# Attention scores on the halves of the PE array: one head of a pair per 64 rows, query-score and key-score matmuls in turn

## The reference

```python
x = x + layernorm(attention(layernorm(x)))      # 16 batches, 256 tokens, 16 heads of width 8
x = x + layernorm(ffn(layernorm(x)))            # 32 experts of width 64, top 6, and a shared one of 256
# attention, for each batch and head:
scores = einsum('bhtd,bhsd->bhts', q, k) / sqrt(8)
out = einsum('bhts,bhsd->bhtd', softmax(scores), v)
```

## Time and profile before

| | |
|---|---|
| timed runs, us | 591.12, 585.29, 587.35 |
| median | 587.35 us |
| profiled execution: span from first to last instruction | 588.6 us |
| instructions in it | 10713 |
| mean granted clock of TensorE | 0.986 of full speed |
| attention with its start, feed-forward layer | about 0 to 305 us, 305 to 588 us |

### The profile page before, as it was taken

The page is one execution under the profiler, slowest core; times in us unless marked ns, Lnnn a source line. Parts: engine busy times, 40 slices in busy tenths (PEclk is TensorE's granted clock), DMA queues, the critical chain, the costliest instruction groups (busy, mean ns, idle before and its releaser), DMA issues.

```text
span 588.6 us, 10713 instructions
## 1 busy us (share of the span) xinstructions
PE 541.1 (92%) x3248; PEld 316.9 (54%) x3248; DVE 423.1 (72%) x1116; ACT 430.1 (73%) x879; POOL 191.2 (32%) x763
## 2 busy tenths in 40 slices
PE   2488979999999999999989999999999999999993
PEld 1234545555555555654446565656566566556551
DVE  6686757789887878768856968695876769487343
ACT  2326757788887987877687687887869687877873
POOL 6241111225153424121103335535363553403030
PEclk9999989999998999999999999999999999999997
DMA  6333364333333233223000000000000000000001
GB/s 176 116 101 93 103 233 130 91 95 104 96 102 110 85 110 108 87 87 95 13 3 1 1 1 1 1 19 1 20 0 19 0 3 18 0 19 1 19 0 36
DMA packets 42776, 33.76 MB, mean 57 GB/s; under 512 B 4032, under 2 KB 35392, under 8 KB 42464
## 3 DMA queue, kind: packets, MB, share of 16 engines
q1 hardware_dynamic: 42720, 33.09, 18.8%
HBM read 18.01 MB, written 14.68 MB: 56 GB/s over the span
## 4 chain that ended last, share of the span: by engine, by line
PE 58%; POOL 11%; DMA 6%; issue 6%; ACT 6%; DVE 6%; SPq 6%; ACTq 0%; POOLq 0%; DVEq 0%
PE pY L1183 8%; PE pS L1183 7%; PE pO L1100 7%; PE pS L1088 6%; PE pS L1077 6%; PE pS L1160 4%; PE pS L1162 4%; PE pS L1161 4%; DMA kp<-k_scratch 4%; PE pS L1169 4%; SPq L369 3%; DMA k_scratch<-k_parts 3%; ACT probs L556 2%; SPq L357 2%; DVE mneg L770 2%
## 5 line engine op out<-in xcount | busy, mean ns | idle before, releaser
L770 DVE TENSOR_REDUCE mneg<-pS 128x2 f32<-128x512 f32 x256 | 164.5, 686 | 39.6 <-PE pS L1077 37.8
L556 ACT ACTIVATE probs<-pS 128x512 f32<-128x512 f32 x256 | 140.9, 599 | 46.9 <-PE pS L1088 46.3
L946 DVE TENSOR_TENSOR h_ring<-pS,rr 128x512 f32<-128x512 f32 x128 | 88.4, 691 | 79.4 <-ACT rr L633 74.5
L1077 PE MATMUL pS<-kp,qp 96*128 96x256 bf16 x512 | 103.8, 288 | 11.5 <-DMA kp<-k_scratch 10.8
L624 ACT ACTIVATE r<-pS 128x512 f32<-128x512 f32 x144 | 84.7, 588 | 29.3 <-PE pS L1162 29.1
L1088 PE MATMUL pS<-qp,kp 102*128 102x512 bf16 x256 | 99.8, 393 | 4.7 <-ACT probs L556 3.0
L633 ACT ACTIVATE rr<-r 128x512 f32<-128x512 f32 x128 | 80.8, 631 | 4.4 <-DVE h_ring L946 0.5
L1160 PE MATMUL pS<-qp,up_hi 128*128 128x512 f32 x144 | 80.6, 560 | 0.9 <-ACT r L624 0.8
L1077 PEld LDWEIGHTS pS<-kp,qp 96*128 96x128 bf16 x512 | 45.6, 101 | 58.3 <-issue 16.6
L1183 PE MATMUL pS<-h_ring,down_sb 128*128 128x512 f32 x144 | 73.4, 591 | 0.0
L1183 PE MATMUL pY<-h_ring,down_sb 128*128 128x512 f32 x144 | 72.9, 591 | 0.0
(11 more groups left out here) (191 smaller groups left out, 802.2 us busy)
## 6 DMA issues: line engine op xcount, KB each, us to landing
qp<-q_scratch SPq DMA_DIRECT2D x64, 96.0 KB
kp<-k_scratch SPq DMA_DIRECT2D x64, 96.0 KB
q_scratch<-q_parts SPq DMA_DIRECT2D x16, 192.0 KB, 2.2
k_scratch<-k_parts SPq DMA_DIRECT2D x16, 192.0 KB, 2.2
q_scratch<-q_parts SPq DMA_DIRECT2D x16, 128.0 KB, 2.1
k_scratch<-k_parts SPq DMA_DIRECT2D x16, 128.0 KB, 2.1
out_x<-ot SPq DMA_DIRECT2D x7, 256.0 KB, 2.3
q_scratch<-q_parts SPq DMA_DIRECT2D x16, 64.0 KB, 1.8
```

What stands on the lines that cost most here:

```text
L556: nc.scalar.activation(probs[j][:, sh], pS2[n % S2_RING][:, :, :], ACT.Exp, scale=SCALE).then_inc(exp_done, 1)
L770: nc.vector.tensor_reduce(mneg[u % 2][:, :, hh, k], pS1[n % S1_RING][:, :].rearrange("p (a s) -> p a s", a=TH), AX.X, ALU.max, negate=True ...
L946: nc.vector.tensor_tensor(h_sb[n % HRING], pC[k % 2], r2_sb[k % 2][:, :], ALU.mult).then_inc(h_done, 1)
L1077: ins = mm(pS1[n % S1_RING][:, T * th:T * (th + 1)], qp[slot][0:2 * QK_ROWS, hh, k, P * th:P * (th + 1)], kp[slot][0:2 * QK_ROWS, k, :], s ...
```

## The change

Each head of a pair gets a half of the array's rows: head 0 rows 0 to 47, head 1 rows 64 to 111 (HALF = 64), with the three rows of its maxima behind them, 51 rows in all. `qp` needs no zeroed copies and shrinks to half. A key-score call now covers one head and both halves of the keys in two matmuls of 256 columns, head 1 first (`KEY_HEADS`), and `probs` is laid out accordingly. In each step of a batch but the last one, `scores_by_both` first makes all waits and then issues four matmuls of 256 columns: query scores of one head, key scores of the other head, and both again. The last batch has key scores alone, and the first two units query scores alone, with the heads in turn. POOL's zeroing of `qp` goes; the ones are now written to 32 partitions in each half, so by two DVE instructions for each `kp` buffer. x_lo moves to `kp`, and x_cut gets a tile of its own.

```diff
-DIFF_ROWS = 2 * QK_ROWS + 2 * M_ROWS
+DIFF_ROWS = QK_ROWS + M_ROWS
+HALF = P // 2
+KEY_HEADS = (1, 0)
...
-        qp = [sb(f"qp{i}", [P, 2, UB, T], BF16) for i in range(RING)]
+        qp = [sb(f"qp{i}", [P, UB, T], BF16) for i in range(RING)]
...
-                    rows = slice(QK_ROWS * hh, QK_ROWS * (hh + 1))
+                    rows = slice(HALF * hh, HALF * hh + QK_ROWS)
...
-            sp.wait_ge(preset, 1)
             sp.wait_ge(ones_set, 1)
...
-            for i in range(RING):
-                ins = nc.gpsimd.memset(qp[i][:, :, :, :].rearrange("p a b c -> p (a b c)").bitcast(F32), 0.0)
-            ins.then_inc(preset, 1)
...
-                for sh in range(TH):
-                    n = TH * (NBLK * b + j) + sh
+                for i, hh in enumerate(KEY_HEADS):
+                    n = 2 * (NBLK * b + j) + i
                     act.wait_ge(s2_done, n + 1)
-                    nc.scalar.activation(probs[j][:, sh], pS2[n % S2_RING][:, :, :], ACT.Exp,
+                    nc.scalar.activation(probs[j][:, hh], pS2[n % S2_RING][:, :, :], ACT.Exp,
...
             for i in range(RING - 1):
-                nc.vector.memset(kp[i][2 * QK_ROWS:P, :, :], 1.0)
+                for hh in range(2):
+                    nc.vector.memset(kp[i][HALF * hh + HALF // 2:HALF * (hh + 1), :, :], 1.0)
...
+            def query_scores(u, k, hh, th):
+                slot, n = u % RING, 2 * (UB * u + k) + hh
+                rows = slice(HALF * hh, HALF * hh + QK_ROWS)
+                return mm(pS1[n % S1_RING][:, T * th:T * (th + 1)], qp[slot][rows, k, P * th:P * (th + 1)],
+                          kp[slot][rows, k, :], start=True, stop=True)
+
+            def key_scores(u, k, i, sh):
+                slot, n = u % RING, 2 * (UB * u + k) + i
+                rows = slice(HALF * KEY_HEADS[i], HALF * KEY_HEADS[i] + DIFF_ROWS)
+                return mm(pS2[n % S2_RING][:, sh], kp[slot][rows, k, P * sh:P * (sh + 1)], qp[slot][rows, k, :],
+                          start=True, stop=True)
...
+            def scores_by_both(uq, uk, k, i):
+
+                query_scores_free(uq, k, i)
+                key_scores_free(uk, k, i)
+                query_scores(uq, k, i, 0)
+                key_scores(uk, k, i, 0)
+                query_scores(uq, k, i, 1).then_inc(s1_done, 1)
+                key_scores(uk, k, i, 1).then_inc(s2_done, 1)
...
                         if not last:
-                            scores_by_query(2 * b + 2 + j // UB, j % UB, hh)
-                        scores_by_key(b, j, hh)
+                            scores_by_both(2 * b + 2 + j // UB, 2 * b + j // UB, j % UB, hh)
+                        else:
+                            scores_by_key(2 * b + j // UB, j % UB, hh)
```

More of the change, by code:

```diff
@@ L150, in block_kernel @@
         mT_sb = [sb(f"mT{i}", [2 * M_ROWS * UB, T], BF16) for i in range(2)]
-        probs = [sb(f"probs{j}", [P, TH, 2, T]) for j in range(NBLK)]
+        probs = [sb(f"probs{j}", [P, 2, TH, T]) for j in range(NBLK)]
         oT_sb = sb("oT_sb", [P, 4, T])
@@ L159, in block_kernel @@
         xT = sb("xT", [P, TILE])
-        x_hi, x_lo = ([qp[i][:, part].rearrange("p a b -> p (a b)").bitcast(F32R) for i in range(2)]
-                      for part in range(2))
-        x_cut = kp[0][:, :, :].rearrange("p a b -> p (a b)").bitcast(F32)
+        x_hi, x_lo = ([ring[i][:, :, :].rearrange("p a b -> p (a b)").bitcast(F32R) for i in range(2)]
+                      for ring in (qp, kp))
+        x_cut = sb("x_cut", [P, TILE])
         e_sb = sb("e_sb", [P, C4, E])
@@ L600, in high_x @@
                     act.wait_ge(up_done, FBLK * (i - 1))
-                copy(x_hi[i % 2], x_cut).then_inc(xhi_done, 1)
+                copy(x_hi[i % 2], x_cut[:, :]).then_inc(xhi_done, 1)
             def high_up(c):
@@ L962, in _ @@
             ins.then_inc(ln1_stats, 1)
-            nc.vector.memset(kp[RING - 1][2 * QK_ROWS:P, :, :], 1.0).then_inc(ones_set, 1)
+            for hh in range(2):
+                ins = nc.vector.memset(kp[RING - 1][HALF * hh + HALF // 2:HALF * (hh + 1), :, :], 1.0)
+            ins.then_inc(ones_set, 1)
             dve.wait_ge(wqk_loaded, 16 * N_WQK)
@@ L967, in _ @@
             dve.wait_ge(wa_loaded, 16 * N_WA)
-            dve.wait_ge(preset, 2)
+            dve.wait_ge(preset, 1)
             keep_v(0)
@@ L1072, in scores_by_query, with query_scores_free @@
+            def query_scores_free(u, k, hh):
+                n = 2 * (UB * u + k) + hh
                 if k == 0 and hh == 0:
-                    pe.wait_ge(packed[slot], 4 * 16 * (u // RING + 1))
+                    pe.wait_ge(packed[u % RING], 4 * 16 * (u // RING + 1))
                 if n >= S1_RING:
                     pe.wait_ge(max_done, n - S1_RING + 1)
-                for th in range(TH):
-                    ins = mm(pS1[n % S1_RING][:, T * th:T * (th + 1)], qp[slot][0:2 * QK_ROWS, hh, k, P * th:P * (th + 1)],
-                             kp[slot][0:2 * QK_ROWS, k, :], start=True, stop=True)
@@ L1079, in scores_by_query, with key_scores_free @@
[L1079 to L1085, removed]
+            def key_scores_free(u, k, i):
+                n = 2 * (UB * u + k) + i
+                if k == 0 and i == 0:
+                    pe.wait_ge(m_packed[u % RING], 2 * 16 * (u // RING + 1))
@@ L1086, in scores_by_key, with scores_by_query @@
                 if n >= S2_RING:
                     pe.wait_ge(exp_done, n - S2_RING + 1)
-                mm(pS2[n % S2_RING][:, :, :], kp[slot][0:DIFF_ROWS, k, P * sh:P * (sh + 1)],
-                   qp[slot][0:DIFF_ROWS, :, k, :], start=True, stop=True).then_inc(s2_done, 1)
+            def scores_by_query(u, k):
+                for hh in range(2):
+                    query_scores_free(u, k, hh)
+                for th in range(TH):
+                    for hh in range(2):
+                        ins = query_scores(u, k, hh, th)
+                        if th == TH - 1:
+                            ins.then_inc(s1_done, 1)
@@ new lines, in scores_by_key @@
+            def scores_by_key(u, k, i):
+                key_scores_free(u, k, i)
+                for sh in range(TH):
+                    ins = key_scores(u, k, i, sh)
+                ins.then_inc(s2_done, 1)
+            def scores_by_both(uq, uk, k, i):
[5 more added lines that the diff above has]
+                key_scores(uk, k, i, 1).then_inc(s2_done, 1)
@@ L1204, in _ @@
                 for k in range(UB):
-                    for hh in range(2):
-                        scores_by_query(u, k, hh)
+                    scores_by_query(u, k)
                     if u == 1 and k == 1:
```

13 lines of the change are left out of this document (6 added, 7 removed).

## The result

Forecast 580 us, faster. Measured: 591.24 us (median of four runs, 590.54 to 592.63) against 586.32 for the kernel before in the same session (584.72 to 591.12). The ratio is 1.0091, interval 1.0056 to 1.0125: slower by about 0.9%. The prediction was wrong, and in its sign. The profiled execution ran 591.85 us, with a span of 589.9.

A forecast was written before the change was run, and what follows sets the result against it. PE, busy 541.1 of 588.6 us, was taken as the bound, the DRAM round trip close behind. Start +2.2, batch 2 -1.4, nine batches -8.5, batches 6 to 8 -1.3, clock +1.5: -7.5 from 587.35, so 580; range 570 to 599.

The forecast's parts named there:

- A step halves to 0.23 us: Score matmuls on PE: a step falls from 0.45 to 0.23 us, sixteen steps saving 3.5 us per batch.
- The rival of 603: Halves don't run at once: steps stay at 0.45 us, change-overs add 1.1 us per batch on PE; 603 us, chance 0.16.
- Change-overs of 0.1 us: Between scores and whole-array work on PE: 11 new changes of the array's division, 0.1 us each, 1.1 us per batch.
- Start +2.2: Before the first scores: doubled writes of ones add 3.2 us, dropped zeroing of qp gives back 1.0, net +2.2.
- What ACT and DVE allow with their waits, about 14.2: Attention batches: with the DRAM round trip not binding, a batch falls to about 14.2 us.
- the loop-free rival: The DRAM round trip doesn't bind and loads land sooner: -1.85 us for each of nine batches, 568 us, chance 0.14.
- These make 14.8; with jitter 15.1: Round trip through SP and DRAM: maxima's copy at 2.8 us plus 12.0 to landing sets ordinary batches, 15.1 instead of 16.05.
- a saving of 8.5 us: Nine ordinary batches between 3 and 15: 0.95 us less each, 8.5 us saved.
- The clock, +1.5 with bounds 0 and 8: PE idle at batch starts: three falls of the clock to its lower level add 1.5 us.
- The base: Starting time for the forecast: median of the shown runs, 587.35 us, beside a profiled span of 588.6.
- The rival "the gain is eaten": Landing times over 4 us or clock falls in most batches leave 15.8 us per batch; 587 us, chance 0.20.
- The chance of "slower", 0.19: Whole kernel slower by over 1%: 0.16 from halves not running at once and a little of the eaten case.

The follow-up runs named there:

- e4: Changed kernel with KEY_HEADS = (0, 1), so both scores of a step use the same half of the array: 604.79 us, ratio 1.0336.
- e2: Changed kernel without the DRAM round trip of q and k: no writes after batch 1, loads read parts of batches 0 and 1; 580.65 us, ratio 0.9921.
- h1: e2 with half of the outputs' matmuls left out (8 instead of 16 a call): 584.71 us, one run.
- h3: e2 with ACT's exponentials over half the keys from batch 1 on: 575.54 us, one run.
- g3: e2 with each outputs call cut in two, eight matmuls ahead of the pair's second step and eight behind: 585.63 us, ratio 1.0005.
- f2: e2 with both query matmuls of a step first, then the wait for the exponential and both key matmuls: 582.63 us, ratio 0.9935.

## Why the prediction was wrong, point by point

**A step halves to 0.23 us: right** (0.23 in the timeline, and not the 0.29 given beside it; 0.45 where both matmuls share a half and no other step is at hand). The rival of 603 meets e4's 604.79 by luck: it had PE full with 17.1 us per batch, and e4's PE is busy for 15.3 of 17.3.

**Change-overs of 0.1 us: near.** project_qk's two pairs take 0.54 and 0.52 us from start to start, where each took 0.43 in the kernel before: some 0.2 us for a change there and back. PE's demand of 13.5 us was measured as 13.8 to 13.9.

**Start +2.2: right in sum** (+2.1), in part because two misses cancel. The statistics began at 7.72, not 7.3, because a write now comes every 1.16 us, not every 1.07. The chain of the layer norm was 1.0 us shorter, as forecast, so its last instruction came 2.7 us later than before (11.36 against 8.68), and 0.6 of that was made up before the first exponential.

**"What ACT and DVE allow with their waits, about 14.2": this failed first.** It is 15.4 (e2). I took ACT's 12.7 us and added 1.5 for waits, without going through the ring. PE's 13.9 and ACT's 12.8 us overlap only in part: h1 and h3 show that each engine's time counts, PE's for most and ACT's for a little under half of what is taken from it. That the two key-score banks are too few to bridge the uneven blocks of both (1 us of outputs on PE, copies and norms on ACT) is the likely reason, and it is not shown; splitting the outputs (g3) gained 0.1 us at most. So even with the round trip cut a batch gave 0.5 us, not the 1.85 of the loop-free rival.

**"These make 14.8; with jitter 15.1": this is the term that turned the sign.** In its place the nine batches took 16.4 us on average, so a saving of 8.5 us became a loss of 3.2 between the two profiles. For an undisturbed batch 14.8 is about right. Where PE waited for the load, the next first exponential came 0.75 us after its landing; by that, the load allowed 14.3 us in batch 10 and 15.3 in batch 5. But this sits at or just under a pace of 15.4, where before it sat 1.1 us under 16. I put 0.3 us of jitter on it. The chain that ended last shows what jitter is, in batch 3 of the kernel after:

```profile
97.14 0.36 ACT mT L513
...
101.69 3.93 DMA k_scratch<-k_parts
...
108.03 0.70 SPq L372
...
109.60 2.43 DMA qp<-mT
112.03 0.25 issue
112.27 0.37 PE pS L1075
```

From the start of the last write's issue to landing 3.93 us pass. From the issue of load_max to the first load it is 8.1 us (97.53 to 105.64) instead of 120.41 - 114.42 = 6.0 in the earlier trace rows; the last kp load then lands at 111.69, after the usual 3.7. Late writes are as frequent before: from the start of the last write's issue to the first load pass 3.5 to 4.9 us in batches 0, 1, 2 and 7 there, 3.1 to 4.2 in batches 0, 2, 3 and 9 here, and mostly 1.8 otherwise. What differs is the cover. Batch 7 before took 17.3, 1.5 us over the pace of 15.8; batch 3 here took 17.7, 2.3 over 15.4, and both end where the late load lets them. I had also left out that load_max is issued behind the four loads: its 6 KB landed at 112.03, 0.3 us behind the kp load. PE then waited:

```profile
112.27 0.37 PE L1075 MATMUL pS<-kp,qp 48*128 48x256 bf16 x1 [1.89 <-DMA qp<-mT]
...
114.00 0.37 PE L1075 MATMUL pS<-kp,qp 48*128 48x256 bf16 x1 [0.69 <-ACT probs L555]
```

**The clock, +1.5 with bounds 0 and 8: right in kind, low in size.** The same place in windows of 2 us:

```profile
110.00:112.00 2.00, 0.39 (x8) 0.00 (x0) 1.22 (x3) 0.55 (x2) 0.88 (x4) 0.96 0.21 55
112.00:114.00 2.00, 1.04 (x8) 0.54 (x9) 1.04 (x2) 0.74 (x2) 0.00 (x0) 0.50 0.05 9
114.00:116.00 2.00, 2.00 (x18) 0.75 (x22) 1.44 (x3) 1.99 (x6) 0.97 (x2) 0.50 0.29 100
```

PE works 0.39 us of two, then the granted clock is 0.50, the lower of the two levels (1.2 GHz), and PE is full at half pace. That is batch 4's 17.3 us against batch 5's 15.4: 1.9 us for one fall. I had estimated most of a fall inside PE's new slack; but while it lasts every matmul takes twice as long, and 1.5 us of slack are soon gone. Batches 6 and 14, with one shorter fall each, took 0.9 and 0.8 us more than before. Five batches after batch 0 had clocks of 0.84 to 0.96 here, two in the kernel before.

**The base: wrong by about 3.4 us**, since the profiled span was set beside the median (above). The forecast from 590.7 would have been 583, still faster.

The range of 570 to 599 does hold 591.24, by its width: its upper part was there for the rival of 603.

The rival "the gain is eaten" (587, chance 0.20) had the right two causes, landing time and clock. The chance of "slower", 0.19, was tied to a mechanism that didn't occur; nothing in my list joined the start's cost with an attention that gains nothing, which gives 590 by my own terms.

What stays open: why in some batches a write to DRAM lands 2 us late, and the share of the clock alone in the 10.6 us that the round trip costs, since no run held the clock fixed; and whether a third key-score bank would free the 15.4.

## What to carry to other kernels

When an engine is 99% busy and two others 80%, ask what the waits between them leave before promising the 20%: make each engine lighter in turn, and see which one the period follows. A loop that passed unseen 1 us under the old bound becomes the bound when that falls by 0.5, and it brings its scatter along: judge it by its late cases, not its mean. Work taken from TensorE can come back as idle time at the next wait and then as half clock, as in batch 4 here; the runs do not say how much lighter is too light. And a run made to stand for a rival has to be read in its trace: e4 came within 2 us of the rival's time by another mechanism.

## What the runs showed of the hardware

- Two matmuls in different 64-row halves started in the same 10 ns: four of 256 columns took 0.23 us in pairs, 0.45 in series.
- TensorE started matmuls of the other half ahead of the kernel's order: in e4 two steps of different halves ran at once, eight matmuls in 0.56 us; in f2 a key matmul started 0.07 us before a query matmul that the kernel issues ahead of it.
- A DVE write of 1024 bf16 elements per partition took 0.91 us over 32 partitions and over 128.
- 0.39 us of matmuls in 2 us stood ahead of a fall of the granted clock to 0.50, which made a batch 1.9 us longer. With 1.5 to 2 us per batch less of TensorE's work, one run (h1) had ten batches at mean granted clocks of 0.63 to 0.82 and was no faster than its parent.
- The clock's record can begin late: before 46.3 us the trace of before gives 1.00, while its matmuls took 409 ns instead of 274.
- Small DVE instructions on 128 x 2 elements took 0.16 to 0.17 us alone, and up to 0.78 while POOL wrote.
